# Sixteen-wide attentions on one NeuronCore: dividing by the softmax sums before the turn instead of after the value products, half-width outputs, and a new order table

## What is computed

```
x = L0(x, ctx)   # causal self attention (0), cross attention (1), each: LN(x + z * mask); then ReLU MLP, LN
x = L1(x, ctx)   # RMS norm, rotary grouped attention (2), Wo, residual; RMS norm, SwiGLU MLP, residual
x = L2(x, ctx)   # LN of both sides, attention (3) with biases, residual + out @ Wo + bo   (no LN after)
x = L3(x, ctx)   # attention (4): scores * (0.5 mask + 0.5), clipped to +-50, softmax, Wo, residual, LN
# every attention:  out = softmax(q k^T / sqrt(hd)) v
```

## Time and profile before

| | |
|---|---|
| device time, median of 3 runs | 4097.45 us (4096.05 to 4101.04) |
| device time of the profiled execution | 4097.15 us |
| span of the profiled execution | 4095.3 us |
| PE / PEld busy | 3961.5 us (97%) / 3439.0 us (84%) |
| DVE / ACT / POOL busy | 2890.5 us (71%) / 2659.4 us (65%) / 1231.2 us (30%) |
| mean granted TensorE clock | 0.989 of full speed |

### The profile page before, as it was taken

One profiled execution on the slowest core, in us unless ns is written; L12 is line 12 of the kernel. 1 busy time (PEld: TensorE's weight loads), 2 busy tenths in 40 slices (PEclk: granted clock), 3 DMA queues, 4 the chain that ended last, 5 costly groups with the idle time before them and its releaser, 6 DMA issues.

```text
span 4095.3 us, 115148 instructions
## 1 busy us (share of the span) xinstructions
PE 3961.5 (97%) x44448; PEld 3439.0 (84%) x44448; DVE 2890.5 (71%) x10721; ACT 2659.4 (65%) x8449; POOL 1231.2 (30%) x2247
## 2 busy tenths in 40 slices
PE   5999999999999999999999999999999999999997
PEld 5888888888888888888888888888888888888885
DVE  4667777777777777777777777777777777777763
ACT  2666666666666666666666666666666666666663
POOL 1233233332332332333332332323323323323331
PEclk7999999999999999999999999999999999999997
DMA  3000000000000000000000000000000000000000
GB/s 143 2 17 17 10 17 17 10 17 17 9 17 16 10 17 9 17 17 9 17 17 9 17 17 10 17 17 10 17 17 10 17 12 14 17 9 17 17 3 5
DMA packets 66495, 69.61 MB, mean 17 GB/s; under 512 B 7456, under 2 KB 64800, under 8 KB 65056
## 3 DMA queue, kind: packets, MB, share of 16 engines
q1 hardware_dynamic: 65952, 62.25, 4.8%
HBM read 53.83 MB, written 8.39 MB: 15 GB/s over the span
## 4 chain that ended last, share of the span: by engine, by line
PE 55%; DVE 32%; issue 7%; POOL 3%; ACT 3%; DMA 1%; SPq 0%; DVEq 0%; POOLq 0%; ACTq 0%
PE gen_ps L467 34%; PE gen_ps L459 10%; DVE masked L971 4%; DVE negmax L977 4%; PE scores_ps L549 3%; PE gen_ps L601 3%; DVE st L937 2%; DVE zn L932 2%; DVE masked L964 2%; PE gen_ps L589 2%; PE scores_ps L556 2%; PE scores_ps L563 2%; POOL rstd L788 1%; POOL res L796 1%; DVE rdenm L929 1%
## 5 line engine op out<-in xcount | busy, mean ns | idle before, releaser
L467 PE MATMUL gen_ps<-actT,w_sb 128*128 128x128 f32 x10752 | 1390.1, 279 | 28.9 <-DVE wide L1110 13.5
L467 PEld LDWEIGHTS gen_ps<-actT,w_sb 128*128 128x128 f32 x10752 | 1285.8, 192 | 107.2 <-issue 51.5
L699 ACT ACTIVATE probT<-gen_ps 128x512 f32<-128x512 f32 x1024 | 585.5, 642 | 293.8 <-PE gen_ps L459 293.8
L788 POOL TENSOR_TENSOR rstd<-ve,consts 128x1 f32<-128x1 f32 x448 | 282.6, 631 | 1521.2 <-DVE ve L939 772.1
L733 ACT ACTIVATE prob<-scores_ps,negmax 128x128 f32<-128x128 f32 x2048 | 561.6, 432 | 189.3 <-DVE negmax L977 189.3
L459 PE MATMUL gen_ps<-consts,prob 128*128 128x128 f32 x4096 | 594.4, 278 | 16.1 <-ACT prob L733 6.4
L459 PEld LDWEIGHTS gen_ps<-consts,prob 128*128 128x128 f32 x4096 | 469.8, 142 | 129.2 <-ACT prob L733 58.2
L699 ACT ACTIVATE actT<-gen_ps 128x256 f32<-128x256 f32 (+1 forms) x512 | 235.7, 460 | 383.8 <-PE gen_ps L459 377.3
L467 PE MATMUL gen_ps<-w_sb,actT 128*128 128x256 f32 x1792 | 465.4, 383 | 3.8 <-ACT actT L699 2.8
L849 POOL TENSOR_SCALAR prob<-prob,rden 128x128 f32<-128x128 f32 x1024 | 358.8, 372 | 358.6 <-DVE rden L1050 358.6
L467 PE MATMUL gen_ps<-w_sb,wide 128*128 128x256 f32 x2056 | 465.7, 379 | 0.8 <-DVE wide L1117 0.4
(11 more groups left out here) (116 smaller groups left out, 6053.0 us busy)
## 6 DMA issues: line engine op xcount, KB each, us to landing
actT<-xT_dram SPq DMA_DIRECT2D x64, 128.0 KB, 2.2
ctx_rms<-x_dram SPq DMA_DIRECT2D x64, 128.0 KB, 2.2
ctx<-ctx_dram SPq DMA_DIRECT2D x64, 128.0 KB, 2.3
ctxT<-ctxT_dram SPq DMA_DIRECT2D x64, 128.0 KB, 2.3
mask<-mask_dram SPq DMA_DIRECT2D x128, 64.0 KB, 2.1
out_dram<-res SPq DMA_DIRECT2D x64, 128.0 KB, 1.7
w_sb<-weights_dram SPq DMA_DIRECT2D x2, 2048.0 KB, 18.6
w_sb<-weights_dram SPq DMA_DIRECT2D x2, 1024.0 KB, 20.2
```

Of the source, the lines that this page charges most:

```text
L467: last = nc.tensor.matmul(ps, lhsT(c), rhs(c), start=(c == 0), stop=(c == chunks - 1))
L699: release(nc.scalar.activation(dst, take(act, name, b)[:, 0:width], ACT.Copy), name, b)
L788: nc.gpsimd.tensor_tensor(dst, src, const("expo")[:, 0:width], ALU.pow)\
```

## The change

Attentions 0, 1 and 3 now do what attention 2 did: their exponentials also write the sums (`accum_out`), and the probabilities are divided before `turn`. For attention 2 the multiplication stays on POOL; for 0, 1 and 3 DVE does reciprocal and multiplication, one [128, 512] operation per unit, 12 units a round. Then the ones column isn't needed, and two heads share a block of 32 rows: `v16` holds a pair of heads as [v_even, 0, 0, v_odd], the first matmul uses its columns 0 to 31 and the second, which accumulates on the same rows, its columns 32 to 63. The number of value matmuls is unchanged; the result is [128, 256]. In attentions 0 and 1 two transposes instead of four turn it back, and DVE does mask and residual in one operation (`add_attended`), which takes POOL's addition away. In attention 3 the result is already what `o` needs, so `attended` and `zT` are gone for it: ACT copies it right into `actT`. Attention 4 keeps the ones column, now in a buffer of its own, `v4`, in a part of `wide` that is free at that time; POOL writes the columns 16 to 31 anew for each sequence (`tail4`). `norm_x4` is written as a `scalar_tensor_tensor` with a broadcast operand. POOL's `ctx_norms` also waits for `res_0`. And the whole table is new, `BANK_LATE` (a switch of where in a step PE waits for its bank) is empty.

```diff
-PERIOD = 71.632128
+PERIOD = 83.308747
...
-BANK_LATE = {"t32", "t33"}
+BANK_LATE = set()
+NORM_ON_GPSIMD = [2]
...
 def turn(a, b, u):
-                if a == 2:
-                    pe.wait_ge(sem("normed"), U * b + u + 1)
-                else:
-                    pe.wait_ge(sem("exp_done"), N + 1)
+                pe.wait_ge(sem(f"normed_{a}"), U * b + u + 1)
...
 def values(a, b):
+                if a == 4:
+                    pe.wait_ge(sem("tail4"), b + 1)
...
-                for u in range(U):
-                    for k in range(HU):
-                        last = nc.tensor.matmul(ps[32 * k:32 * k + 32, u * S:(u + 1) * S],
-                                                v16[:, b % G, HU * u + k, :], probT[:, u, k, :],
-                                                start=True, stop=True)
+                    for c in range(C):
+                        for e in range(2):
+                            for k in range(HU):
+                                j = HU * c + k
+                                last = nc.tensor.matmul(ps[32 * k:32 * k + 32, c * S:(c + 1) * S],
+                                                        v16[:, b % G, j, VW * e:VW * (e + 1)],
+                                                        probT[:, j // 2, 2 * (j % 2) + e, :],
+                                                        start=(e == 0), stop=(e == 1))
...
-                    transposes(f"on{a}", b, [oT[:, PLACE_OF[a, b] % 2, u, :] for u in range(U)])
+                    transposes(f"on{a}", b, [oT[:, PLACE_OF[a, b] % 2, u, :] for u in range(U if a == 4 else C)])
...
 def exponentials(a, b, u):
-                                                   bias=negmax[:, N % 4, k:k + 1])
+                                                   bias=negmax[:, N % 4, k:k + 1], accum_out=den[:, N % 4, k:k + 1])
...
 # ACT, values
+                    if a == 3:
+                        copy_out("v3", b, flat(actT[:, g, 0:2, :]), D)
...
+                        width = 2 * D if a == 4 else D
+                        copy_out(f"v{a}", b, flat(oT[:, place % 2, :, :])[:, 0:width], width)
...
 # DVE, new
+            def add_attended(a, b):
+                ps = take(dve, f"on{a}", b)
+                nc.vector.scalar_tensor_tensor(res[:, g, :], ps[:, 0:D], live[:, a, g:g + 1],
+                                               (xs if a else x_in)[:, g, :], ALU.mult, ALU.add)\
+                    .then_inc(sem(f"res_{a}"), 1)
+                dve.wait_ge(sem(f"res_{a}"), b + 1)
+                release(nc.vector.nop(), f"on{a}", b)
...
 # DVE, prob_norm
-                    nc.vector.reciprocal(rden2[:, N % 4, :], den[:, N % 4, :]).then_inc(sem("rden2"), 1)
+                    if a in NORM_ON_GPSIMD:
+                        nc.vector.reciprocal(rden2[:, N % 4, :], den[:, N % 4, :]).then_inc(sem(f"rden2_{a}"), 1)
+                    else:
+                        link(nc.vector.reciprocal(rden2[:, N % 4, :], den[:, N % 4, :]))
+                        nc.vector.tensor_tensor(prob[:, N % 4, :, :], prob[:, N % 4, :, :],
+                                                rden2[:, N % 4, :].unsqueeze(2).to_broadcast([P, HU, S]), ALU.mult)\
+                            .then_inc(sem(f"normed_{a}"), 1)
...
 # POOL, new
+                elif name == "tail4":
+                    nc.gpsimd.tensor_copy(v4[:, g, :, 16:32], const("tail").unsqueeze(1).to_broadcast([P, H, 16]))\
+                        .then_inc(sem("tail4"), 1)
...
 # DVE, norm_x4
-                    nc.vector.tensor_scalar(zn[:, g, :], xs[:, g, :], mv[:, g, 0:1], rstd[:, g, 0:1],
-                                            ALU.subtract, ALU.mult).then_inc(sem("n4"), 1)
+                    nc.vector.scalar_tensor_tensor(zn[:, g, :], xs[:, g, :], mv[:, g, 0:1],
+                                                   rstd[:, g, 0:1].to_broadcast([P, D]), ALU.subtract,
+                                                   ALU.mult).then_inc(sem("n4"), 1)
```

More of the change, by code:

```diff
@@ new lines @@
+    ("queries", 0, 0, {"PE": 0.000, "DVE": 63.990}),
+    ("keys", 0, 0, {"PE": 0.629, "ACT": 36.313}),
+    ("first_row", 0, 0, {"PE": 13.920, "DVE": 74.051}),
+    ("scores", 0, 0, {"PE": 32.505}),
+    ("turn", 0, 0, {"PE": 39.747, "ACT": 72.053}),
+    ("turn", 0, 1, {"PE": 43.000, "ACT": 74.226}),
+    ("stats", 0, 0, {"DVE": 129.429, "POOL": 43.214}),
+    ("norm", 0, 0, {"DVE": 129.610, "POOL": 51.670}),
+    ("rows_in", 0, 0, {"DVE": 62.379}),
+    ("turn", 0, 2, {"PE": 67.325, "ACT": 93.269}),
@@ new lines @@
+    ("turn", 0, 3, {"PE": 68.180, "ACT": 96.552}),
+    ("soft", 0, 0, {"ACT": 68.296, "DVE": 89.094}),
+    ("soft", 0, 1, {"ACT": 69.772, "DVE": 90.346}),
+    ("soft", 0, 2, {"ACT": 70.469, "DVE": 93.255}),
+    ("values", 0, 0, {"PE": 70.685, "ACT": 102.063}),
+    ("soft", 0, 3, {"ACT": 70.903, "DVE": 94.667}),
+    ("ctx_norms", 0, 0, {"DVE": 154.695, "POOL": 73.047}),
+    ("attended", 0, 0, {"PE": 75.644, "DVE": 128.905}),
+    ("tr", 1, 0, {"PE": 79.915, "ACT": 112.256}),
+    ("queries", 1, 0, {"PE": 82.441, "DVE": 143.459}),
@@ new lines @@
+    ("keys", 1, 0, {"PE": 82.593, "ACT": 115.213}),
+    ("first_row", 1, 0, {"PE": 83.881, "DVE": 145.888}),
+    ("scores", 1, 0, {"PE": 86.270}),
+    ("stats", 1, 0, {"DVE": 167.506, "POOL": 86.445}),
+    ("prob_norm", 0, 0, {"DVE": 94.784}),
+    ("prob_norm", 0, 1, {"DVE": 95.264}),
+    ("turn", 1, 0, {"PE": 97.006, "ACT": 128.208}),
+    ("turn", 1, 1, {"PE": 97.791, "ACT": 133.224}),
+    ("prob_norm", 0, 2, {"DVE": 98.298}),
+    ("turn", 1, 2, {"PE": 98.420, "ACT": 138.617}),
+    ("turn", 1, 3, {"PE": 99.559, "ACT": 139.698}),
@@ new lines @@
+    ("tr", 4, 0, {"PE": 249.395, "ACT": 284.170}),
+    ("soft", 3, 0, {"ACT": 254.423, "DVE": 280.450}),
+    ("queries", 4, 0, {"PE": 256.188, "DVE": 317.915}),
+    ("soft", 3, 1, {"ACT": 260.099, "DVE": 280.862}),
+    ("keys", 4, 0, {"PE": 262.031, "ACT": 292.839}),
+    ("soft", 3, 2, {"ACT": 263.097, "DVE": 282.068}),
+    ("norm_x4", 3, 0, {"DVE": 267.503}),
+    ("soft", 3, 3, {"ACT": 267.508, "DVE": 289.402}),
+    ("scores", 4, 0, {"PE": 271.153}),
+    ("prob_norm", 3, 0, {"DVE": 289.510}),
@@ L178 @@
+    ("soft", 4, 3, {"ACT": 314.714, "DVE": 330.685}),
+    ("norm", 4, 0, {"DVE": 380.376}),
 ]
@@ L270, in build @@
         plainT = sb("plainT", [P, G, C, P])
[L271 removed]
+        v16 = sb("v16", [P, G, H // 2, 2 * VW])
         v64 = sb("v64", [P, G, NKV, HD])
```

284 lines of the change are left out of this document (128 added, 156 removed).

## The result

The changed kernel takes 4133.22 us (median of 4 runs, 4132.44 to 4137.34) against 4097.96 in the same comparison: ratio 1.0087, 95% interval 1.007 to 1.0105. It is slower by 0.9%, where 4046 and faster was forecast; the time lies inside the range.

What follows compares the result with a forecast made beforehand. PE was taken as the bound in the steady part. Its -1.2 us a round plus 0.4 of extra idle gave -0.8, a 61.3 us round; with fill and drain at 0, 4046 us, range 4008 to 4150.

Steps and rivals of the forecast that it cites:

- PE loses 1.2 us a round: On PE: 10 fewer transposes a round, 1.09 us, plus 0.1 for no longer waiting for zn; value matmuls counted as unchanged.
- rival 5: On PE: the accumulating value matmuls don't overlap, +7.5 us a round, time 4500; chance 0.03.
- DVE's work: On DVE: 12 reciprocals and multiplications add 9.8 us a round, removals give back 2.1, net +7.7, from 46.8 to 54.5.
- ACT's sums: On ACT: 48 exponentials a round also write sums, 0.09 us each, 4.3 us in all (up to 6.4), beside PE's work.
- norm_x4: On DVE: this step takes 0.81 us because it waits for POOL, and would take about 0.5, so -0.3.
- Fill and drain: Start and end of the run, 122.8 us before: change counted as 0, bounds -10 to +10 us.
- the port's paragraph: SBUF port shared by DVE and POOL: whoever is second waits; bounds nothing, about +1.0 or +2.5 us a round.
- My 0.4 above: Extra PE idle per round, 0.4 us on top of the old 0.8, because PE's and DVE's limits lie close together.
- the two limits of 60.9 and 60.6: Round limits in us: PE's own work, 60.9, and the loop over DVE and PE, 60.5 to 60.7.
- the whole stretch from soft4 to norm0: Part of DVE's list, 35.8 us of work, forming with PE's 22.8 us and handovers a 59.4 us loop before further waits.
- Rival 3: The shared port costs about 1 us and eats the gain: round 61.8 to 62.2, 4078 to 4106; chance 0.15.
- rival 4: Port held for the whole POOL operation: loop 63.1 us, PE waits before turn3.3 and tr1, 4163 (4106 to 4180); chance 0.22.

Runs made afterwards that it cites:

- the kernel with the maximum: Changed kernel with DVE's multiplication of the probabilities replaced by a maximum over the same 128x512 (one SBUF operand, division left out): 4051.82 us, ratio 0.9894.
- Relief ahead of soft3: Changed kernel with the multiplication of attention 0's probabilities moved from DVE to POOL, DVE keeping the reciprocals: 4129.91 us, ratio 1.0083.

## Why the prediction was wrong

- **PE loses 1.2 us a round.** Held, by the waits that show: 61.45 - 60.27 = 1.18. The accumulating value matmuls take 1.0 us for 32, as before (2033.75 to the next group at 2034.77 in a round of after), so rival 5 is out.
- **DVE's work.** The multiplication is 0.69 long and 0.60 from start to start, as taken. The wait for o2 fell to 44.2 us over 63 rounds (2 to 3 us a round forecast, 0.7 measured), so the room was used further than I thought.
- **ACT's sums.** From PSUM one exponential to the next is 0.34 us, 0.07 to 0.09 over the 0.255 to 0.27 without a sum. Without multiplications the kernel is 89 us faster than before, so ACT's time was hidden there.
- **norm_x4 was mis-sized.** I gave it 0.5 instead of 0.81. It takes 0.95, beside POOL's L881 (0.80), and 0.89 even in the kernel with the maximum: it still starts 0.13 us after POOL's addition, and PE waits 0.5 to 0.6 for it before z in every new kernel. With the maximum that is the largest of the visible waits, 0.53 of 1.17; no run changed it alone, so what it costs is open.
- **Fill and drain.** 4131.5 - 64 x 62.59 = 125.7, 2.9 over the 122.8.
- **The step that failed** is in the port's paragraph: "My 0.4 above holds the case near the lower end". The 0.4 us of extra waiting was needed without the port (PE's visible waits with the maximum are 1.17 a round, 0.56 over the 0.61 of before): with the maximum, which takes the same time on DVE as an undisturbed multiplication and leaves POOL's operations at 1.29, the round is 61.30, the forecast's 61.3, and the time 4052. The port came on top with 62.59 - 61.30 = 1.29 us a round, inside the bounds of 1.0 and 2.5 that I had written and not put into the sum. Unit 3.1 comes ahead of POOL and pays nothing; 3.2 pays 0.87, 3.3 pays 0.29, and POOL's two operations are held up by 0.5 each. -1.2 + 0.4 + 1.3 = +0.5. That the round without the port came out at the forecast's own 61.3 is in part luck: of the two limits of 60.9 and 60.6 behind it the second was too short. The round still moves with DVE's piece at 61.30, and the 1.16 us of blocking in 3.2 and 3.3 came to 62.59, where the loop of 60.6 gives 61.8 with them.
- **Why it counts in full** was right in kind and too wide. I took the whole stretch from soft4 to norm0 as the loop. Relief ahead of soft3 gave nothing (4130), and the round follows the length of the piece from the last row maximum of attention 3 to attended0's addition nearly one for one. kv2's bank, which attended0's transposes take, has 66.4 us of PE's waiting in the changed kernel; that wait was missing from the argument, but reading the bank sooner gave nothing.
- **Rival 3** (gain eaten, port about 1 us) is the nearest in mechanism, **rival 4** in sign; its waits before turn 3.3 and tr1 came as 0.16 and 0.48, and the largest was before attended0. The Trainium skill's rule (SBUF — State Buffer, Who interferes with whom), that the second of the two blocks until the first is through, is what the rows of 3.2 show: 1.56 us, ending 0.6 after POOL's 1.80. The rule is borne out; rival 4's count of who comes second was not: it charged 3.1 and 3.2 with about 1 us each and 3.3 and norm_x4 with 0.3, and 3.1 paid nothing.

Open: the 55.4 us outside the piece were never changed on purpose, so which of PE's steps in them close the loop is argued from the lists and not shown.

## What to carry to other kernels

When work is added to DVE as an operation with two SBUF operands, list the POOL operations that read SBUF and are released just ahead of it, and charge the rest of the POOL operation to the sum, not to the range. Then look for the piece of DVE's list whose length the round follows one for one, and judge an edit by what it does to that piece: here moving keys inside it changed only which of PE's steps waited, and relief outside it changed nothing. A PE wait with a large total names where the loss shows, not what to repair. What helped was to give one unit of the piece's work to an engine with idle time; with two units PE waited for that engine.
